# The value projection of a fused attention and gate kernel, taken as seven products of quarters

## What is computed

```python
def reference(x, ...):                       # x: 4 x 1024 x 1024, float32
    xn = layernorm(x)
    h = rmsnorm(xn, qkv_norm_w)
    q, k, v = h @ ternary(qkv_w).T           # 16 heads of 64
    # by chunks of 128 tokens, state S per head:
    scores = (q @ k.T) * mask                # decays with distance
    o = scale * (scores @ v + (q * lam_t) @ S)
    S = lam_T * S + (k * lam_rev).T @ v
    s = rmsnorm(rmsnorm(o, norm_w), proj_norm_w) @ ternary(proj_w).T
    g = silu(xn @ ternary(weight).T + bias)
    return x + s * g
```

## Time and profile before

| | |
|---|---|
| median of 3 runs | 1390.45 us (1390.08 to 1390.53) |
| profiled execution | 1392.01 us |
| its span, first to last instruction | 1390.8 us |
| PE busy | 1362.5 us, 98% of the span |
| DVE busy | 811.8 us, 58% |
| POOL busy | 573.2 us, 41% |
| ACT busy | 443.2 us, 32% |
| PE's share of the chain that ended last | 88% |

### The profile page before, as it was taken

The page is one execution under the profiler, slowest core; times in us unless marked ns, Lnnn a source line. Parts: engine busy times, 40 slices in busy tenths (PEclk is TensorE's granted clock), DMA queues, the critical chain, the costliest instruction groups (busy, mean ns, idle before and its releaser), DMA issues.

```text
span 1390.8 us, 27028 instructions
## 1 busy us (share of the span) xinstructions
PE 1362.5 (98%) x11425; PEld 939.5 (68%) x11425; DVE 811.8 (58%) x1323; ACT 443.2 (32%) x780; POOL 573.2 (41%) x524
## 2 busy tenths in 40 slices
PE   5999999999999999999999999999999999999998
PEld 2677677676676767668576676767668576676765
DVE  7885373664637548374564737548364674736634
ACT  5883232232322323232232323223232232323311
POOL 1524633433515354344432624345244433634332
PEclk9999999999999999999999999999999999999999
DMA  9521102112030110301102030110301102020000
GB/s 363 212 91 62 35 5 67 33 34 63 6 95 5 61 39 1 95 5 62 39 21 76 5 94 6 62 40 1 95 5 61 39 16 82 5 81 20 16 16 31
DMA packets 27770, 74.67 MB, mean 54 GB/s; under 512 B 6913, under 2 KB 10753, under 8 KB 27650
## 3 DMA queue, kind: packets, MB, share of 16 engines
q1 hardware_dynamic: 27360, 72.92, 16.8%
q10 hardware_dynamic: 290, 0.02, 0.0%
HBM read 56.12 MB, written 16.81 MB: 52 GB/s over the span
## 4 chain that ended last, share of the span: by engine, by line
PE 88%; POOL 4%; DVE 3%; ACT 2%; issue 2%; DMA 1%; SPq 0%; POOLq 0%; ACTq 0%; DVEq 0%
PE ring L549 32%; PE ring L666 15%; PE ring L561 14%; PE ring L534 11%; PE att_ps L584 4%; PE att_ps L624 3%; PE att_ps L628 3%; PE att_ps L606 2%; PE ring L592 1%; POOL arena L1628 1%; PE ring L511 1%; DMA raw<-in_ffn_w 1%; ACT junk L1304 1%; PE ring L646 1%; PE ring L654 1%
## 5 line engine op out<-in xcount | busy, mean ns | idle before, releaser
L549 PE MATMUL ring<-b_hi,qkv_q 128*128 128x256 f16 x2048 | 452.8, 273 | 0.0
L549 PE MATMUL ring<-b_lo,qkv_q 128*128 128x256 f16 x2048 | 452.7, 273 | 0.0
L549 PEld LDWEIGHTS ring<-b_hi,qkv_q 128*128 128x128 fp8e4 x2048 | 202.1, 99 | 28.2
L549 PEld LDWEIGHTS ring<-b_lo,qkv_q 128*128 128x128 fp8e4 x2048 | 200.7, 98 | 28.5
L561 PE MATMUL ring<-qkv_q,b_hi 128*128 128x512 fp8e4 x512 | 194.3, 380 | 0.0
L561 PE MATMUL ring<-qkv_q,b_lo 128*128 128x512 fp8e4 x512 | 194.0, 379 | 0.0
L666 PE MATMUL ring<-proj_q,o_hi 128*128 128x512 fp8e4 x496 | 188.1, 379 | 2.9 <-DVE o_lo L1099 2.7
L666 PE MATMUL ring<-proj_q,o_lo 128*128 128x512 fp8e4 x496 | 188.0, 379 | 0.0
L1038 DVE TENSOR_TENSOR arena<-att_ps,mask 128x512 f32<-128x512 f32 x128 | 79.5, 683 | 89.8 <-PE att_ps L584 89.8
L1407 ACT ACTIVATE arena<-ring,wscale 128x512 f32<-128x512 f32 x64 | 44.0, 687 | 258.4 <-PE ring L549 258.4
L1624 POOL TENSOR_TENSOR arena<-arena,cols 128x1024 f32<-128x1024 f32 x29 | 55.0, 1897 | 150.5 <-ACT arena L1426 150.5
(11 more groups left out here) (192 smaller groups left out, 2346.0 us busy)
## 6 DMA issues: line engine op xcount, KB each, us to landing
xt<-in_x SPq DMA_DIRECT2D x32, 512.0 KB, 3.5
out<-xt SPq DMA_DIRECT2D x31, 512.0 KB, 5.0
raw<-in_qkv_w SPq DMA_DIRECT2D x24, 512.0 KB, 15.7
y<-in_x_turned SPq DMA_DIRECT2D x14, 512.0 KB, 4.0
y_odd<-in_x_turned SPq DMA_DIRECT2D x14, 512.0 KB, 5.3
raw<-in_ffn_w SPq DMA_DIRECT2D x8, 512.0 KB, 9.8
norm_rows<-norm_out SPq DMA_DIRECT2D x28, 128.0 KB, 3.9
raw<-in_proj_w SPq DMA_DIRECT2D x6, 512.0 KB, 4.4
```

What stands on the lines that cost most here:

```text
L549: ins = pe.matmul(ring[:, b, e * BT:(e + 1) * BT], qkv_q[:, cb, o:o + P], part[:, cb, :], start=(cb == 0 and part is b_hi), stop=(cb == NC ...
```

## The change

From block 2 on v of the block's two chunks (256 tokens x 1024 by 1024 x 1024) is also taken by quarters: seven `v_product` of eight matmuls in place of four `project_v` of 16. Five of them stand ahead of chunk 0's scores, p7 and p4 behind, among the ffn's. For this:

- ACT makes `b` itself in float32 (`weigh_b`, 16 instructions in a block), into the place where the masked scores stand later; DVE sums its quarters (`sum_b`, 4), ACT makes high parts of the sums (4) and DVE low parts (`low_b_sum`, 4).
- v's quarters are put together by ACT (`begin_v_bank`, `begin_v`, `take_v`: 5 instructions, where `v_out` had 4) and DVE (`add_v`, 2).
- POOL makes four sums of v's weights once, in block 2 (`sum_v_weights`).
- `sq` moves out of the arena into its own place.
- The ffn's p2 and p7 move behind chunk 0's `update_state`, p4 to chunk 1.
- `high_b` of chunk 0 moves ahead of the attention; that of chunk 1 moves behind `square_o` of chunk 1.
- On DVE `centre` of chunk 1 and the last three quarters of `split_b` move behind `weight_o` and `add_state`.
- POOL's `sum_squares` of chunk 1 waits for the next block's last `b_lo`.

```diff
@@ tensor_program
+            def v_product(i, name):
+                if (i, name) == (2, "p1"):
+                    pe.wait_ge(s_vwsum, 4)
+                part, weights = FACTORS[name]
+                if part in Y_SUMS:
+                    pe.wait_ge(s_bslo, of_b_sum(i, part))
+                if name in ("p1", "p5"):
+                    b = free_bank("v product", i, name)
+                else:
+                    b = bank_of("v product", i, SHARED[name])
+                if name in ("p2", "p6"):
+                    pe.wait_ge(s_vseed, i - 1)
+                elif name == "p3":
+                    pe.wait_ge(s_vbase, 2 * (i - 2) + 1)
+                elif name == "p7":
+                    pe.wait_ge(s_vbase, 2 * (i - 2) + 2)
+                elif name == "p4":
+                    pe.wait_ge(s_vsum, of_pair(i, 1))
+                for j in range(CPH):
+                    for k, of in enumerate(b_part_of(part)):
+                        ins = pe.matmul(ring[:, b, :], of[:, j, :], v_weights_of(weights)[:, j, :],
...
@@ attention, PE
                 elif i > 1 and c == 0:
+                    v_product(i, "p7")
                     product(i, "p1")
+                    v_product(i, "p4")
                     product(i, "p6")
-                    product(i, "p2")
-                    product(i, "p7")
-                elif i > 1 and last:
-                    product(i, "p5")
-                    project_v(i, 1, 1)
                 elif i > 1:
-                    project_v(i, 1, 1)
+                    product(i, "p4")
                     product(i, "p5")
...
-                if i > 1:
-                    product(i, "p3" if c == 1 else "p4")
+                if i > 1 and c == 1:
+                    product(i, "p3")
...
+                    elif i == 1:
+                        project_v(1, 1, 1)
                     else:
-                        project_v(i, 1, 0 if i > 1 else 1)
+                        product(i, "p2")
+                        product(i, "p7")
...
-                    project_v(i, 0, 0)
-                    project_v(i, 0, 1)
+                elif i > 1:
+                    v_product(i, "p1")
+                    v_product(i, "p5")
+                    v_product(i, "p2")
+                    v_product(i, "p6")
+                    v_product(i, "p3")
@@ sum_y, DVE
                 if name == "S1":
-
                     dve.wait_ge(s_blo, of_half(i, 1, 1))
+                    dve.wait_ge(s_bw, of_pair(i, 1))
@@ attention, DVE
+                    add_v(i, 1)
                     begin_z12(i)
+                if more and c == 0 and i > 0:
+                    norm_stats(i + 1, 1)
+                if i > 1 and c == 0:
                     go_on_z12(i)
-                    take_z11(i)
-                    go_on_z22(i)
                 if c == 1:
-                    if i > 1 and last:
-                        take_z22(i)
-                    if more and i > 1:
-                        centre(i + 1, 1)
-                    if i > 1 and not last:
+                    if i > 1:
+                        take_z21(i)
                         take_z22(i)
                     output_scale(i, 0)
...
-                    elif more:
-                        if i == 1:
-                            centre(2, 1)
-                        split_b(i + 1, 0, 1)
-                    if more:
-                        split_b(i + 1, 1, 0)
-                        split_b(i + 1, 1, 1)
+                        split_b(1, 1, 0)
+                        split_b(1, 1, 1)
                 weight_o(i, c, 0)
                 weight_o(i, c, 1)
                 if not last:
...
+                    elif i > 1:
+                        take_z11(i)
+                        go_on_z22(i)
                 else:
+                    if more and i > 0:
+                        split_b(i + 1, 0, 1)
+                        centre(i + 1, 1)
                     gate_out(i, 0, 0)
+                    if more and i > 0:
+                        split_b(i + 1, 1, 0)
+                        split_b(i + 1, 1, 1)
@@ scalar_program
+            def weigh_b(i, c):
+                act.wait_ge(s_o, HALF * (chunk(i - 1, 1) + 1))
+                act.wait_ge(s_yn, of_turned(i, c))
+                for cb in range(NCB):
+                    ins = act.activation(b_turned[:, c, cb, :], y_turned[c][:, cb, :], ACT.Copy, scale=cols[:, 0, cb:cb + 1])
+                ins.then_inc(s_bw, 1)
...
+                elif more and i > 0:
+                    high_b(i + 1, 1, 0)
+                    high_b(i + 1, 1, 1)
@@ gpsimd_program
                     output_scale(i, 0)
+                    if more and i > 0:
+
+                        pool.wait_ge(s_blo, of_half(i + 1, 1, 1))
                     sum_squares(i, 1)
...
+                    elif i == 2:
+                        for name in ("T1", "T2", "T4", "T3"):
+                            sum_v_weights(name)
                     add_out(i - 1, 1, 0)
```

More of the change, by code:

```diff
@@ L91, in program @@
         arena = sb("arena", [P, ARENA])
+        SQ = 2 * PR * T
+        with nc.sbuf_tensor("sq", [P, 2, PR, T], F32) as sq:
+            pass
+        b_sum_hi = sb("b_sum_hi", [P, 4, CPH, T], F16)
+        b_sum_lo = sb("b_sum_lo", [P, 4, CPH, T], F16)
         ow = sb("ow", [P, PR, T])
@@ L361, in program @@
                 elif i > 1:
-                    ring_uses += [("product", i, "p5"), ("v", i, 1, 1)][::1 if last else -1]
+                    ring_uses.append(("product", i, "p5"))
                 if c == 1:
@@ L939, in sum_y, with sum_b, low_b_sum, add_v @@
                 dve.tensor_tensor(y_of(name), y_of(one), y_of(other), op).then_inc(s_ysum, 1)
+            def sum_b(i, name):
+                one, other, op = {"S1": ("a21", "a22", ALU.add), "S3": ("a11", "a21", ALU.subtract),
+                                  "S2": ("S1", "a11", ALU.subtract), "S4": ("a12", "S2", ALU.subtract)}[name]
+                dve.wait_ge(s_bw, of_pair(i, 1))
+                if of_b_sum(i, name) > 1:
+                    dve.wait_ge(s_bsum, of_b_sum(i, name) - 1)
+                dve.tensor_tensor(b_of_quarter(name), b_of_quarter(one), b_of_quarter(other), op).then_inc(s_bsum, 1)
+            def low_b_sum(i, name):
+                hi, lo = b_part_of(name)
+                dve.wait_ge(s_bshi, of_b_sum(i, name))
+                dve.tensor_tensor(lo, b_of_quarter(name), hi, ALU.subtract).then_inc(s_bslo, 1)
+            def add_v(i, c):
+                dve.wait_ge(s_vps, of_v_product(i, "p7" if c else "p3"))
+                dve.wait_ge(s_vbase, 2 * (i - 2) + (1 if c else 2))
+                v = v_tok[:, c, BANK:C]
+                dve.scalar_tensor_tensor(out=v, in0=ring[:, bank_of("v product", i, "p6" if c else "p5"), :],
+                                         scalar=wscale[:, 7:8], in1=v, op0=ALU.mult, op1=ALU.add).then_inc(s_vsum, 1)
             def take_b(i, c, half):
@@ L1154, in attention @@
                     normalise(1, 0, again=True)
-                elif more and c == 0:
-                    norm_stats(i + 1, 1)
-                if i > 1 and c == 0:
-                    take_z21(i)
                 if c == 1:
@@ L1287, in vector_program @@
                         centre(i + 1, 0)
+                    if i > 1:
+                        add_v(i, 0)
                 attention(i, 0)
@@ L1355, in high_part, with high_b_sum, begin_v_bank, begin_v @@
                 act.activation(part_of(name)[0], y_of(name), ACT.Copy).then_inc(s_ahi, 1)
+            def weigh_b(i, c):
[4 more added lines that the diff above has]
+                ins.then_inc(s_bw, 1)
+            def high_b_sum(i, name):
+                if name == "S1":
+                    act.wait_ge(s_red, sums(chunk(i - 1, 1)))
+                act.wait_ge(s_bsum, of_b_sum(i, name))
+                act.activation(b_part_of(name)[0], b_of_quarter(name), ACT.Copy).then_inc(s_bshi, 1)
+            def begin_v_bank(i):
+                act.wait_ge(s_vps, of_v_product(i, "p1"))
+                act.wait_ge(*emptied_before("v product", i, "p6"))
+                act.activation(ring[:, bank_of("v product", i, "p6"), :], ring[:, bank_of("v product", i, "p1"), :],
+                               ACT.Copy).then_inc(s_vseed, 1)
+            def begin_v(i, c):
+                act.wait_ge(s_vps, of_v_product(i, "p5" if c else "p6"))
+                act.activation(v_tok[:, c, BANK:C], ring[:, bank_of("v product", i, "p5" if c else "p6"), :],
+                               ACT.Copy, scale=wscale[:, 7:8]).then_inc(s_vbase, 1)
+            def take_v(i, c):
+                act.wait_ge(s_vps, of_v_product(i, "p4" if c else "p2"))
+                act.activation(v_tok[:, c, 0:BANK], ring[:, bank_of("v product", i, "p6" if c else "p1"), :],
+                               ACT.Copy, scale=wscale[:, 7:8]).then_inc(s_v, 1)
             def base_z(i):
@@ L1524, in scalar_program @@
                     high_part(i, "a12")
+                    weigh_b(i, 0)
```

(13 more changed lines are left out.)

125 lines of the change are left out of this document (97 added, 28 removed).

## The result

The changed kernel takes **1431.57 us** (median of 4 runs, 1430.90 to 1432.04), the kernel before 1390.49 beside it (1390.08 to 1392.77): a ratio of 1.0292, with a 95% interval of 1.0274 to 1.0309. It is slower by 41 us. The profiled execution took 1432.04 with a span of 1430.8, 40.0 above the span before.

A forecast was written before the change was run, and what follows sets the result against it. The prediction took PE, busy for 98% of the span, as the bound. Its terms, -24.2 + 30.1 + 18.2 + 1 + 10 + 2.4 = +37.5 us, on the median of 1390.45 gave 1427 us, with a range of 1398 to 1438.

The forecast's parts named there:

- What is removed, -24.2: PE in blocks 2 to 15: 112 fewer matmuls of v at 0.2158 us each, saving 24.2 us.
- The end of a block, +30.1: PE waits for DVE's late b_lo, 2.6 us in ten blocks and 1.4 in three: +30.1 us.
- The start of a block, +18.2: Starts of blocks 3 to 15: 1.4 us each for POOL's late chain or a slow clock, not added: +18.2 us.
- The end of block 1 and start of block 2, +1: Block 1's late b_lo makes PE resume about 1 us later; block 2's start keeps its old losses: +1 us.
- PE resumes about 1 us later than it did: End of block 1: b_lo done near 204.4 instead of 200.7, costing PE about 1 us.
- Has them again: Start of block 2: both old losses, 1.69 + 1.6 = 3.3 us, recur for other reasons.
- Block 2, +10: DVE's low parts and split_o each wait for one of POOL's weight sums, holding PE: +10 us, bounds 0 and 13.
- the row at 792.00: A trace row lasting 1.81 us under a POOL sum, where another of its size takes 0.74; basis for block 2's 10 us.
- the other reading: Block 2: if DVE and POOL shared bandwidth instead of excluding each other, the cost would be 2 or 3 us.
- the upper bound: Block 2: 13 us, allowing for a slow clock once more behind the wait.
- Small or hidden, +2.4: PE waits 0.6 us for take_z22 before p3 in the last blocks of four sequences: +2.4 us; other items hidden.

The follow-up runs named there:

- e5: e4 with three of v's weight sums held until DVE has centred block 2's chunk 0, the fourth behind add_out in block 2: 1365.65 us.
- e1: The changed kernel with chunk 1's centre and the last low parts moved ahead on DVE, and ACT's high parts ahead of the squares: 1387.16 us.
- e7: The kernel before with only the change's late order of centre, low and high parts and POOL's wait, v as before: 1443.21 us.
- e3: The changed kernel with POOL making the output's scale ahead of chunk 0's two output additions: 1424.87 us.
- e2: The changed kernel with POOL's four sums of v's weights made in block 1 instead of block 2: 1417.96 us.
- e8: e5 with four further POOL sums of the weights' shape in block 2, whose result nothing reads: 1377.70 us.
- e9: The changed kernel with each of the four weight sums cut into four POOL instructions: 1419.49 us.
- e6: The changed kernel without POOL's wait for b_lo ahead of chunk 1's squares: 1510.00 us.
- e4: The changed kernel with the edits of e1, e2 and e3 together: 1370.91 us.
- e10: e5 without POOL's wait for b_lo ahead of the squares: 1365.20 us.

## Why the prediction was right

Slower was right, and 1431.57 lies in the range of 1398 to 1438, 4.6 above the forecast of 1427. Of the 4.6, 2.5 are the sum itself (+37.5 against +40.0 on the span); the rest is that the profiled execution stood 1.6 above its median before and 0.5 above it now, and that the sum's 1427.95 was put at 1427. By its steps:

- **What is removed, -24.2.** There are 112 matmuls less. e5 shows the block without waits: 82.43 us where the kernel before has 84.42. Of these 1.99, eight matmuls are 1.73. Of the other 0.26, `turn_k` is one half (its 16 matmuls take 1.88 where they took 2.01), and the other is that the products' matmuls stand a little closer together; why, no run shows.
- **The end of a block, +30.1.** Right. PE's 33.6 us less the 2.92 of block 1 are 30.7; a hold was 2.6 in ten blocks and 1.47 in three, with 2.6 and 1.4 predicted. e1 and e7 show this from both sides.
- **The start of a block, +18.2.** The amount is right, 18.2 over 13 starts against the +10.84 of the kernel before: 7 x 1.17 with POOL late and 6 x 1.66 with the clock down. That the two don't add was argued and is shown by e3. What was wrong is the picture behind a single value: the clock fell at about half of the starts, neither always nor never. That this mixture has the mean of 1.4 that I took for POOL's lateness alone is luck.
- **The end of block 1 and start of block 2, +1.** The amount was right by luck, and both its steps were wrong. "PE resumes about 1 us later than it did" was 4.0: the block starts at 205.60 and not at 201.57, of which 2.92 is the hold and about 1 was there before the first scores, where the two programs are alike. "Has them again" was wrong the other way: `spread_gamma` comes at +12.5, not at the +14.4 of the kernel before, since POOL's squares and the slow stretch now overlap. -1.9 and +2.9 leave +1.0.
- **Block 2, +10.** 10.45 measured, by the mechanism of the row at 792.00: e2 takes it away, e8 makes it without any data, e9 scales it with the length of one POOL instruction. The step that was short is the clock behind this wait: ten matmuls about 0.2 us too slow, 2.0 us, which I had put in the upper bound only. These 2.0, the 1 us from before the first scores, 0.6 at the block ends and 0.45 here make 4.1 over the sum; the span shows 2.5. The other 1.6, a tenth of a microsecond a block, fits the small gain of the first point, which isn't in the sum.
- **Small or hidden, +2.4.** 2.4 in 4, as predicted. The other items cost nothing that shows in PE's waits.

Two pages of the Trainium skill were weighed. The rule of "SBUF — State Buffer", section "Who interferes with whom", held as read: 0.68 us became 4.30, and the sum by the other reading (2 or 3 us for block 2) would have missed the 10.45. On the clock, "TensorE: Matmul & The Clock Gate", section "What's actually happening", has the throttled clock as the default. I drew from it that a wait of 2.6 us is apt to be followed by a slow stretch each time; that step was mine, the section does not say it of such a wait. These traces say otherwise. Counting the holds at `b_lo` in the changed kernel, e2, e3, e7 and e9 together: after 1.47 us none of 15 was followed by a slow stretch, after 2.6 to 2.9 us 35 of 55 were; in e6, after 6.1 to 8.1 us, each of the 14 was. What decides among the 55 is open.

The larger misses among the expectations, beside e1's 5 us, are all of one kind: e4 (5 us), e6 (35 to 60 us) and e10 (15 us or more the other way). Each time I had priced the rule correctly for the instructions I was watching and not asked which others of DVE stand under the POOL instruction (e4), how many they are (e6), or when POOL's would really begin (e10).

Not tried: whether POOL instructions that only write, such as a fill, hold DVE as well.

## What to carry to other kernels

Saved matmuls count only if each engine's last delivery to PE stays early: find what the next stage's first matmul needs, and let DVE and ACT make that before work whose reader is later (here this order alone was worth 44 us, the products 24). Put long GpSimd instructions where VectorE has nothing urgent to do on two SBUF tiles, or cut them short; and when VectorE's durations vary for one shape, lay GpSimd's timeline beside them before counting bytes or semaphores. When two losses fall into the same stretch, price the larger, and when a wait on an engine looks needless, take it away in the final order, not in another.
